# Row sums from a column of ones in v, mixing into two banks, transposes in two halves through one bank, and another order at the beginning

## The reference

```python
x = x + tanh(g_xattn) * attention(layernorm(x), ctx)
#   q = Wq.x + bq, k = Wk.ctx + bk, v = Wv.ctx + bv     (128 channels = 8 heads of 16)
#   each of the 1024 positions looks at a window of 16 positions around it;
#   dots = q.k_win * 16**-0.5, softmax over the window, out = sum of attn * v_win, then Wo.out + bo
x = x + tanh(g_ffn) * ffn(layernorm(x))
#   silu(x.G) * (x.U) . D, with G, U (1024, 3584) and D (3584, 1024) integers of 0 to 15,
#   less a zero point and times a scale for each group of 128 rows
```

## Time and profile before

| | |
|---|---|
| median of 3 runs | 1634.97 us (1632.92 to 1637.67) |
| profiled execution | 1636.69 us, its span 1634.9 us |
| busy, of the span | PE 95%, DVE 89%, ACT 64%, POOL 79% |
| chain that ended last | PE 88%, issue 3%, POOL 2%, SP queue 2% |
| mean granted clock of PE | 0.989 |

### The profile page before, as it was taken

How to read it: one execution, slowest core, us unless ns; L and a number is a source line. 1 busy time by engine, 2 the same in 40 slices (tenths; PEclk the granted TensorE clock), 3 DMA queues, 4 the chain that set the end, 5 groups by cost and what they waited for, 6 DMA issues and landing times.

```text
span 1634.9 us, 40568 instructions
## 1 busy us (share of the span) xinstructions
PE 1554.2 (95%) x16614; PEld 810.4 (50%) x16614; DVE 1455.4 (89%) x1429; ACT 1049.9 (64%) x1187; POOL 1288.5 (79%) x945
## 2 busy tenths in 40 slices
PE   5899999998789999999999999999999999999996
PEld 3566666676434444444444444444444444444444
DVE  4688878887599999999999999999999999999997
ACT  4577777776456666666666666666666666666652
POOL 3576766776778888888888888888888888888865
PEclk9899999999899999999999999999999999999999
DMA  4666655655366766666666666666666776667579
GB/s 120 152 157 146 174 136 148 175 146 131 104 155 155 153 154 148 152 153 153 152 152 153 153 155 155 155 154 150 153 149 147 156 155 152 152 154 155 116 180 322
DMA packets 193139, 252.66 MB, mean 155 GB/s; under 512 B 14542, under 2 KB 138126, under 8 KB 192938
## 3 DMA queue, kind: packets, MB, share of 16 engines
q1 hardware_dynamic: 168186, 163.74, 35.1%
q0 software_dynamic: 23616, 85.99, 30.0%
q10 hardware_dynamic: 1152, 0.33, 0.1%
HBM read 113.92 MB, written 16.78 MB: 80 GB/s over the span
## 4 chain that ended last, share of the span: by engine, by line
PE 88%; issue 3%; POOL 2%; SPq 2%; DMA 1%; DVE 1%; ACT 1%; ACTq 0%; DVEq 0%; POOLq 0%
PE bank L1189 68%; PE bank L1098 3%; PE bank L1087 3%; PE bank L1130 2%; PE bank L1050 2%; PE bank L1061 2%; PE bank L1046 2%; PE bank L1054 2%; PE bank L1108 1%; PE bank L1077 1%; PE bank L1058 1%; PE bank L1066 1%; POOL oacc L618 1%; SPq L392 1%; DMA gates<-in_g_ffn_dram 1%
## 5 line engine op out<-in xcount | busy, mean ns | idle before, releaser
L974 DVE SCALAR_TENSOR_TENSOR acc<-bank,scale,acc 128x1024 f32<-128x1024 f32 x784 | 969.8, 1279 | 49.6 <-PE bank L1189 10.8
L1189 PE MATMUL bank<-xT,w_int 128*128 128x512 f16 x3584 | 846.4, 379 | 10.2 <-DVE xT L925 4.6
L618 POOL TENSOR_TENSOR oacc<-oacc,d_part 128x1024 f32<-128x1024 f32 x225 | 550.4, 2450 | 55.4 <-ACT d_part L811 49.3
L1189 PEld LDWEIGHTS bank<-xT,w_int 128*128 128x128 f16 x3584 | 349.9, 98 | 434.5 <-DVE xT L925 6.2
L811 ACT ACTIVATE d_part<-bank,scale 128x1024 f32<-128x1024 f32 x225 | 250.9, 1115 | 205.3 <-PE bank L1189 201.3
L1189 PE MATMUL bank<-h_hi,d_int 128*128 128x512 f16 x896 | 339.6, 379 | 3.8 <-ACT acc L785 1.8
L1189 PE MATMUL bank<-h_lo,d_int 128*128 128x512 f16 x896 | 339.6, 379 | 0.0
L811 ACT ACTIVATE d_more<-bank,scale 128x1024 f32<-128x1024 f32 x164 | 182.8, 1115 | 156.2 <-PE bank L1189 156.2
L620 POOL DMA_DIRECT2D oacc<-d_more x164 | 155.0, 945 | 116.2 <-ACT d_more L811 109.9
L560 POOL TENSOR_TENSOR raw_z<-raw_w,raw_z 128x512 int32<-128x512 int32 x168 | 225.2, 1341 | 8.8 <-DMA raw_z<-in_L_ffn_gate_z_dram 5.3
L686 ACT ACTIVATE pT<-bank 96x1024 f16<-96x1024 f16 x128 | 123.5, 1018 | 32.8 <-PE bank L1098 32.4
(11 more groups left out here) (86 smaller groups left out, 1512.6 us busy)
## 6 DMA issues: line engine op xcount, KB each, us to landing
oacc<-d_more POOLq DMA_DIRECT2D x164, 512.0 KB, 5.0
raw_w<-in_L_ffn_gate_w_dram SPq DMA_DIRECT2D x56, 256.0 KB, 3.6
raw_z<-in_L_ffn_gate_z_dram SPq DMA_DIRECT2D x56, 256.0 KB, 4.3
raw_w<-in_L_ffn_up_w_dram SPq DMA_DIRECT2D x56, 256.0 KB, 3.4
raw_z<-in_L_ffn_up_z_dram SPq DMA_DIRECT2D x56, 256.0 KB, 4.0
raw_w<-in_L_ffn_down_w_dram SPq DMA_DIRECT2D x56, 256.0 KB, 3.0
raw_z<-in_L_ffn_down_z_dram SPq DMA_DIRECT2D x56, 256.0 KB, 3.7
vt<-vn_hl SPq DMA_DIRECT2D x64, 192.0 KB
```

Source lines behind the costliest of these rows:

```text
L618: nc.gpsimd.tensor_tensor(into, into, d_part[:, (n - 1) % 2, :], ALU.add).then_inc(d_added, 1)
L974: nc.vector.scalar_tensor_tensor(out=into, in0=pair[u % 4][:, :, :].rearrange("p h r -> p (h r)"), scalar=scale[:, par, i, m, k:k + 1], in ...
L1189: last = nc.tensor.matmul(dst[:, h, :], weights, rows_of(h, part), start=(part == 0), stop=(part == 1))
```

## The change

v gets a 33rd column of ones beside its 16 high and 16 low columns, in vn_hl, vt and the padding, written once by POOL. So mix gives the sums of the probabilities as a 33rd column of its output, which now stands in blocks of 64 columns over two banks (6 and 7). add_up goes, and the reciprocal reads the mixing banks in take_mix. The transposed probabilities share one bank (5): turn_probs, take_pT and their semaphores are split into two halves, the first behind the groups first and second, the second behind third. Bank 4 takes the third place in the ring of proj. DVE takes the low halves of second ahead of take_mix.

At the beginning, SP loads the bias ahead of x(1). ACT normalizes x(0) before it takes tanh of the gates. Four of the eight DMAs that move k of batch 0 are issued by ACT, ahead of the copies of q. PE waits for masks and zeros behind the first projections, and not ahead of them, and turns the scales of the feed-forward part behind scores(0); their copies follow exp(0).

```diff
+    V1 = 2 * HD + 1
+    VS = 64
...
-        vn_hl = sb("vn_hl", [P, NV, HEADS, 2, HD], fp16, att)
+        vn_hl = sb("vn_hl", [P, NV, HEADS, V1], fp16, att)
...
-        proj, score, mixed = (bank[0], bank[1], bank[7]), bank[2:4], bank[6]
-        turned = [half[:, :].bitcast(fp16) for half in bank[4:6]]
+        proj, score, mixed = (bank[0], bank[1], bank[4]), bank[2:4], bank[6:8]
+        turned = bank[5][:, :].bitcast(fp16)
         all_scores = pair[1][:, :, 0:JQ * KW].rearrange("p n (j k) -> p n j k", k=KW)
-        all_mixed = mixed[:, 0:JG * HEADS * 2 * HD].rearrange("p (x a d) -> p x a d", a=2, d=HD)
+        all_mixed = pair[3][:, :, :].rearrange("p g (h e) -> p (g h) e", e=VS)
...
             load_ctx(0)
-            load_x(1)
             for n, v in enumerate((bq, bk, bo)):
                 sp.dma_start(bias[:, n:n + 1], v.rearrange("(p a) -> p a", a=1)).then_inc(bias_loaded, 16)
+            load_x(1)
             for m, v in enumerate((gate_s, up_s)):
                 sp.dma_start(gu_stage[m * NK:(m + 1) * NK, 0:F], v).then_inc(s_loaded, 16)
             sp.dma_start(d_stage[0:F // P, :], down_s).then_inc(s_loaded, 16)
-            move_k(0)
+            move_k(0, (0,))
             load_ctx(1)
+            sp.wait_ge(ones_placed, 2)
             place_v(0)
             place_pads()
...
+            nc.gpsimd.memset(vn_hl[:, :, :, 2 * HD], 1.0).then_inc(ones_placed, 1)
+            nc.gpsimd.memset(v_pad[:, :, 2 * HD], 1.0).then_inc(ones_placed, 1)
...
-                    pool.wait_ge(probs_turned, n - 1)
+                    pool.wait_ge(probs_turned, 2 * (n - 1))
...
-            def take_pT(n):
-                act.wait_ge(probs_turned, n + 1)
-                for hg in range(2):
-                    last = nc.scalar.activation(pT[0:2 * KW, n % 2, hg, :], turned[hg][0:2 * KW, :], ACT.Copy)
-                last.then_inc(pT_ready, 1)
+            def take_pT(n, hg):
+
+                act.wait_ge(probs_turned, 2 * n + hg + 1)
+                nc.scalar.activation(pT[0:2 * KW, n % 2, hg, :], turned[0:2 * KW, :], ACT.Copy).then_inc(pT_ready, 1)
...
-            act.wait_ge(gates_loaded, 32)
-            nc.scalar.activation(tanh_g[:, :], gates[:, :], ACT.Tanh).then_inc(gates_ready, 1)
             norm_x(0)
             act.wait_ge(bias_loaded, 48)
-            for t in first_tasks[:4]:
+            for t in first_tasks[:2]:
+                take_high(*t)
+
+            act.wait_ge(emptied_proj, low_done("k", 0, 1))
+            act.wait_ge(km_zeroed[0], 1)
+            for h in range(HG):
+                lo = GC + HD * h
+                act.dma_start(km[0][lo:lo + HD, :, h, PAD:PAD + T], k_hl[lo:lo + HD, :, :]).then_inc(k_moved, 16)
+            for t in first_tasks[2:4]:
                 take_high(*t)
             act.wait_ge(bv_loaded, 16)
-            nc.scalar.activation(v_pad[:, :, 0, :], bv_all.rearrange("p (h d) -> p h d", d=HD), ACT.Copy, scale=-1.0)\
+            nc.scalar.activation(v_pad[:, :, 0:HD], bv_all.rearrange("p (h d) -> p h d", d=HD), ACT.Copy, scale=-1.0)\
                 .then_inc(pad_hi, 1)
             for t in first_tasks[4:]:
                 take_high(*t)
+            act.wait_ge(gates_loaded, 32)
+            nc.scalar.activation(tanh_g[:, :], gates[:, :], ACT.Tanh).then_inc(gates_ready, 1)
...
-                    for t in second + third:
+                    if n == 0:
+                        keep_scales()
+                    for t in second:
                         take_high(*t)
                     if n:
-                        take_pT(n - 1)
+                        take_pT(n - 1, 0)
+                    for t in third:
+                        take_high(*t)
+                    if n:
+                        take_pT(n - 1, 1)
...
-                if n >= 3:
-                    invert_sums(n - 3)
...
-                nc.vector.tensor_reduce(o_sum[:, n % 2], all_mixed.rearrange("p x a d -> p x d a"), AX.X, ALU.add)\
-                    .then_inc(mix_taken, 1)
+                nc.vector.reciprocal(rinv[:, n % 2], all_mixed[:, :, 2 * HD]).then_inc(sums_inverted, 1)
+                nc.vector.tensor_reduce(o_sum[:, n % 2], all_mixed[:, :, 0:2 * HD].rearrange("p x (a d) -> p x d a", a=2),
+                                        AX.X, ALU.add).then_inc(mix_taken, 1)
...
-                    for t in first:
+                    for t in first + second:
                         take_low(*t)
                     if n >= 2:
                         take_mix(n - 2)
-                    for t in second + third:
+                    for t in third:
...
-            def turn_probs(n):
+            def turn_probs(n, hg):
+
                 pe.wait_ge(p_lo, n + 1)
-                if n:
-                    pe.wait_ge(pT_ready, n)
-                for hg in range(2):
-                    for x in range(JQ):
-                        at = (hg * JQ + x) * 2 * KW
-                        last = nc.tensor.transpose(turned[hg][:, x * P:(x + 1) * P], p_hl[:, n % 2, at:at + P], ident16[:, :])
+                if n or hg:
+                    pe.wait_ge(pT_ready, 2 * n + hg)
+                for x in range(JQ):
+                    at = (hg * JQ + x) * 2 * KW
+                    last = nc.tensor.transpose(turned[:, x * P:(x + 1) * P], p_hl[:, n % 2, at:at + P], ident16[:, :])
                 last.then_inc(probs_turned, 1)
-
-            def add_up(n):
-
-                pe.wait_ge(pT_ready, n + 1)
-                for jg in range(JG):
-                    for h in range(HEADS):
-                        x = jg * HEADS + h
-                        at = (jg * HG + h % HG) * P
-                        last = nc.tensor.matmul(sums_at(n)[:, x:x + 1], pT[0:2 * KW, n % 2, h // HG, at:at + P],
-                                                ones16[0:2 * KW, :], start=True, stop=True, skip_group_check=True)
-                last.then_inc(sums_ready, 1)
...
-                pe.wait_ge(pT_ready, n + 1)
+                pe.wait_ge(pT_ready, 2 * n + 2)
                 if n:
                     pe.wait_ge(mix_taken, n)
                 for jg in range(JG):
                     for h in range(HEADS):
-                        to = (jg * HEADS + h) * 2 * HD
                         for jj in range(JJ):
                             c = slice(QB * jj, QB * jj + QB)
                             at = (jg * HG + h % HG) * P + QB * jj
-                            last = nc.tensor.matmul(
-                                mixed[c, to:to + 2 * HD], pT[0:2 * KW, n % 2, h // HG, at:at + QB],
-                                vt[b % 2][0:2 * KW, slot_of(JQ * s + JJ * jg + jj), h].rearrange("p a d -> p (a d)"),
-                                start=True, stop=True)
+                            last = nc.tensor.matmul(mixed[jg][c, VS * h:VS * h + V1], pT[0:2 * KW, n % 2, h // HG, at:at + QB],
+                                                    vt[b % 2][0:2 * KW, slot_of(JQ * s + JJ * jg + jj), h, :],
+                                                    start=True, stop=True)
                 last.then_inc(mix_ready, 1)
...
                     if n:
                         pe.wait_ge(shifted, n)
-                    if n >= 3:
-                        add_up(n - 3)
                     scores(b, s)
+                    if n == 0:
+                        turn_scales()
                     first, second, third = tasks_of(b, s)
                     for t in first + second:
                         project(*t)
+                    if n == 1:
+                        pe.wait_ge(s_kept, 2)
+                    if n:
+                        turn_probs(n - 1, 0)
                     if n >= 2:
                         mix(n - 2)
                     for t in third:
                         project(*t)
-                    if n == 1:
-                        pe.wait_ge(s_kept, 2)
                     if n:
-                        turn_probs(n - 1)
+                        turn_probs(n - 1, 1)
```

More of the change, by code:

```diff
@@ L136, in flamingo_layer @@
         bv_all = xr[:, 0:C]
-        v_pad = xr[:, C:2 * C].bitcast(fp16).rearrange("p (h a d) -> p h a d", a=2, d=HD)
+        v_pad = xr[:, C:C + HEADS * V1 // 2].bitcast(fp16).rearrange("p (h e) -> p h e", e=V1)
         V_MOVES = 16 * 2 * (VW + 2)
@@ L389, in move_k @@
                 for h in range(HG):
-                    for hg in range(2):
+                    for hg in halves:
                         lo = GC * hg + HD * h
@@ L736, in _, with keep_scales @@
                 take_high(*t)
+            act.wait_ge(gates_loaded, 32)
+            nc.scalar.activation(tanh_g[:, :], gates[:, :], ACT.Tanh).then_inc(gates_ready, 1)
             act.wait_ge(gates_ready, 1)
             act.wait_ge(bias_turned, 1)
[L739 removed]
+            nc.scalar.activation(bo_sum[:, :], mixed[0][:, 0:1], ACT.Identity, bias=bias[:, 2:3]).then_inc(bias_summed, 1)
             act.wait_ge(bias_summed, 1)
```

(36 more changed lines are left out.)

51 lines of the change are left out of this document (13 added, 38 removed).

## The result

The changed kernel takes 1668.17 us (1666.13 to 1673.15, 4 runs) against 1634.52 us (4 runs): ratio 1.0196, 95% interval 1.0173 to 1.022, so about 2% slower. In a second session the ratio was 1.0176 (1.0139 to 1.0212). The forecast was 1656 us, in a range of 1642 to 1677.

What follows compares the result with a forecast made beforehand. PE was taken to bound the kernel (88% of the chain), SyncE's queue the opening. Attention +26, batch 1 -1, opening -4, end 0: +21, so 1657.7 us for the profiled execution, 1656 as a median, range 1642 to 1677.

Steps and rivals of the forecast that it cites:

- A: First of four steps (s = 0) of an attention batch: norm_x ahead of exp delays the half copy; forecast 7.3 us.
- B: Second step (s = 1) of an attention batch: its maximum waits behind the row moments; forecast 7.0 us against 5.50.
- C: Third step (s = 2) of an attention batch: no moments ahead of the maximum; forecast 6.03 us against 5.57.
- D: Fourth step (s = 3) of an attention batch: no second copy on ACT; 5.55 to 6.3 us, taken as 6.0.
- The +2.0 per batch: Attention batches: the new wait lengthens each from 24.29 to 26.3 us, +26 us over 13 batches.
- The loop: Attention steps: scores, maximum, subtraction, exp, second copies, half copy, second-half transposes; 6.80 us in B before 0.2 for moments.
- a rival at 0.15: Attention waits: PE's clock falls, 1.5 us each; one fall per batch adds 20 us, giving 1676; chance 0.15.
- the -4 of the sum: Opening: k moves earlier through two queues, so the ctx load lands near 50 instead of 54 us; -4 us.
- 26 us in all, if PE alone sets the pace: Attention steps: removing 64 x 16 one-column sum matmuls saves 0.41 us a step, 1.6 a batch.
- the rival at 1605: Attention: PE alone sets the pace, the half copy is over in time, 26 us go; 1605 us, chance 0.08.
- The end of attention: Batch 15 and the last two steps: A's longer step falls into POOL's weights wait; 0, between -3 and +4 us.

Runs made afterwards that it cites:

- e1: Kernel before with only the transposes in two halves through one bank and their copies in halves: 1681.29 us, ratio 1.028.
- e8: Changed kernel with the transposes' second half moved into the following step, its copy ahead of norm_x and exp: 1630.33 us, 0.9934 of the kernel before.
- e5: The changed kernel itself run again, nothing altered: 1668.71 us.
- e2: Kernel before with only the new opening of the change: 1634.39 us, ratio 0.9996.
- e3: Kernel before without the 1024 one-column sum matmuls, the reciprocal reading a column of ones: 1624.73 us, ratio 0.9922.
- e4: Changed kernel with the first half of the transposes moved up behind the first group and its copy ahead of exp: 1649.66 us, ratio 1.0076.
- e9 to e11: Row moments, inverse_std and norm_row moved later, on the changed kernel, e8 and the kernel before: 1676.47, 1650.34 and 1663.47 us.
- e6: Changed kernel with ACT's first half copy directly behind exp, ahead of the second group's copies: 1669.83 us, ratio 1.0188 to the kernel before.

## Why the prediction was right

**The mechanism.** The new wait is the forecast one: second half of the transposes behind ACT's half copy, behind exp and scores of the same step (52.4 us of waits), and e1 shows it with nothing else of the change in the kernel, at +45 us. The rest of the change then brings this to +34; how much of the 11 us is the sums' is estimated below, and the part of the opening was not seen. e8 shows the other side: with every part of the change but the order of the halves the loss is gone.

**Its size by steps.** Forecast A 7.3, B 7.0, C 6.0, D 6.0, batch 26.3; measured 7.59, 7.16, 6.34, 5.78, batch 26.87. The +2.0 per batch was +2.6 in the trace, 13 x 0.6 = 8 us. That is nearly the whole miss of the profiled execution (1657.7 forecast, 1666.13 measured). The other 4 of the 12 us by which the median lies above 1656 are spread of the runs: the profiled execution stood 2.2 above its median before and 2.0 below it after. The loop itself was sized well. Batches without a fall of the clock take 26.49 (7.56, 6.97, 6.16, 5.80), 0.2 more than forecast; the falls put most of the rest on top. What was mis-sized:
- A: I added 0.7 to a batch of before. But D got shorter by 0.9, and the moments of x at D's end, which end in A, came later as seen from A's masks, so norm_x starts at 3.04 in A instead of 2.66 (each without one batch that stands apart). Against the forecast A is 0.3 longer and D 0.2 shorter, so these two errors nearly cancel, and that is luck.
- C: without a fall the maximum starts at 1.34 and exp at 3.33, where I had 1.35 and 3.28, and C takes 6.16 where I had 6.03. The mean of 6.34 comes from two batches with a low clock (7.15 and 7.22) and one of 6.45.
- The falls of the clock, a rival at 0.15 and the largest error: I had left them out of the sum, and nine came in batches 2 to 14. They cost 0.45 to 1.3 us each where the rival had 1.5 (its 1676), about 6 us in all. In the B shown above the wait at the end is 0.58, where it is 1.71 without a fall (batches 2, 3 and 14), so part of the slow time is taken from the wait. At 1.5 each, nine would have cost 13.5 us and not 6. By the Trainium skill (TensorE: Matmul & The Clock Gate, "What's actually happening") the low clock is the default state and activity lifts it. The granted 0.56 behind the wait agrees, though PE had been busy for 5.66 of the 7.90 us ahead of it.

**The opening.** Forecast was the ctx load at 50 instead of 54, and 4 us:

```profile
50.31 2.05 PE L1054 MATMUL bank<-ct,wk 128*128 128x512 f32 x2 [3.38 <-DMA ct<-in_ctx_dram]
```

In this profile the landing is right against 54.14, and batch 1 started 3.1 earlier. The second profile of the same kernel (e5) does not bear it out:

```profile
52.14 1.10 PE L1054 MATMUL bank<-ct,wk 128*128 128x512 f32 x2 [1.93 <-DMA ct<-in_ctx_dram]
```

Its batch 1 starts at 48.94, no earlier than the 48.80 before. As a time the gain could not be seen (e2), so the -4 of the sum is not shown.

**The sums.** "26 us in all, if PE alone sets the pace" had a condition that does not hold: without the wait the 1024 matmuls are worth 13 us (e3). The forecast's sum did not use the 26, but the rival at 1605 did, and by e3 it was not within reach. With the wait the sums are worth about 12 us as an estimate (0.78 a batch between e1 and the changed kernel); DVE's order and the mixing banks differ between these two as well, and no run parts them. The 33rd column costs nothing that can be seen. Mixing to turning back is 0.63 us here and 0.59 to 0.63 in other steps, where it was 0.60:

```profile
273.97 0.67 PE L1122 MATMUL bank<-vt,pT 96*32 96x33 f16 x64
274.60 0.63 PE L1062 MATMUL bank<-ident,xT 128*128 128x128 f32 x4
```

**The end of attention** was put at 0, between -3 and +4, and was -2.1.

## What to carry to other kernels

A buffer that goes from two to one is paid for by where its release stands in the reader's instruction list: here the copy stood behind work that the waiting engine itself had just issued, which closes a loop through three engines. Write down the loop's length from timeline rows before taking a buffer away; if it is longer than the step, try to put producer and reader of each half in different steps; in e8 the single bank then suffices. When an instruction is moved, look in both directions: for its input (e4), and for who reads its result (e9 to e11). And when means are compared, take the steps with a low clock out first: in e6 they hid a C that was 0.46 us shorter.

## What the runs showed of the hardware that was not expected

- PE's pauses without a releaser are no fixed tax: 22 us before, 4 in the changed kernel, over 40 when mixing is issued twice, nearly all of it in one step of four. All 25 before and all 44 with mixing twice end 1.2 to 1.6 us after a packet of the instruction queue has landed.
- The row "issue" can hide a wait for an engine: in e8 13 of its pieces, 11.8 us, end 0.10 us after a copy of ACT.
- The granted clock fell at waits of 1.5 to 2.4 us that return in every batch (1.86 us, then 0.56 over 3.1 us). In batches 2 to 14 of the kernel before, pauses of up to 1.5 us left it up and only one of 3.2 brought it down. The length of the wait does not decide alone: batch 3 of the changed kernel waited 2.28 us at the end of A and kept its clock, and e1, with 44.4 us of such waits, had four falls where the changed kernel had ten.
